# Attention scores and context of single tokens: from 128-wide block-diagonal products to 32 by 32 products in runs

## The reference, cut to what matters

```python
x = hidden                                     # (1, 2048, 1024)
n = layernorm(x)
q = (n @ wq.T + bq).reshape(B, S, 32, 32)      # k and v alike
scores = einsum('bshd,bstd->bsht', q, k) / sqrt(32)
context = einsum('bsht,bstd->bshd', softmax(scores), v).reshape(B, S, 1024)
x = x + context
x = x + ffn(layernorm(x))                      # w1, w2, w3 (2752 wide), each quantized
                                               # to 16 levels per block of 64 and back
```

## Time and profile before

| what | value |
|---|---|
| time, median of 3 runs | 1934.57 us (1934.41 to 1936.26) |
| the profiled execution's own time | 1933.85 us |
| its span | 1932.1 us |
| PE busy | 1883.0 us (97%) |
| DVE busy | 1730.8 us (90%) |
| ACT busy | 1542.4 us (80%) |
| POOL busy | 1256.0 us (65%) |
| one tile of the attention, in the loop | 30.6 to 30.7 us |

### The profile page before, as it was taken

One profiled execution on the slowest core, in us unless ns is written; L12 is line 12 of the kernel. 1 busy time (PEld: TensorE's weight loads), 2 busy tenths in 40 slices (PEclk: granted clock), 3 DMA queues, 4 the chain that ended last, 5 costly groups with the idle time before them and its releaser, 6 DMA issues.

```text
span 1932.1 us, 30875 instructions
## 1 busy us (share of the span) xinstructions
PE 1883.0 (97%) x10326; PEld 1053.0 (55%) x10326; DVE 1730.8 (90%) x1848; ACT 1542.4 (80%) x1779; POOL 1256.0 (65%) x707
## 2 busy tenths in 40 slices
PE   6899999999989999999999999999999999999998
PEld 5688888888764344444444444444444444444443
DVE  6789888888878999999999999999999999999995
ACT  7366757667568899898898998989989899898881
POOL 0134434343464797887877878778788797786971
PEclk9999999999989999999999999999999999999999
DMA  8435545455286422122122122122122122122114
GB/s 316 142 110 171 166 153 177 137 185 155 79 245 157 143 50 61 44 51 58 43 55 54 43 56 50 46 49 60 43 49 60 43 49 60 43 50 55 39 28 186
DMA packets 252861, 181.69 MB, mean 94 GB/s; under 512 B 177792, under 2 KB 220800, under 8 KB 252800
## 3 DMA queue, kind: packets, MB, share of 16 engines
q1 hardware_dynamic: 221600, 167.28, 30.9%
q10 hardware_dynamic: 31200, 13.64, 2.9%
HBM read 114.29 MB, written 24.12 MB: 72 GB/s over the span
## 4 chain that ended last, share of the span: by engine, by line
PE 64%; DVE 1%; issue 0%; DMA 0%; ACT 0%; SPq 0%; POOL 0%; DVEq 0%
PE bank L1907 42%; PE bank L1935 7%; PE bank L1936 7%; PE bank L1937 7%; PE bank L1933 0%; PE bank L1932 0%; DVE bank L1746 0%; DMA w3T_lo<-half 0%; DVE acc L1811 0%; DVE bank L1744 0%; SPq L1396 0%; DVE w_first L1746 0%; ACT half L1625 0%; ACT signs L1612 0%; DVE hidden L1754 0%
## 5 line engine op out<-in xcount | busy, mean ns | idle before, releaser
L1746 DVE SCALAR_TENSOR_TENSOR bank<-signs,bank 128x1024 f32<-128x1024 int8 (+2 forms) x756 | 920.3, 1217 | 54.6 <-ACT signs L1612 27.9
L1907 PE MATMUL bank<-x2T,w12T 128*128 128x512 f16 x4128 | 906.2, 380 | 11.9 <-DMA x2T<-x_lo_dram 9.0
L1907 PEld LDWEIGHTS bank<-x2T,w12T 128*128 128x128 f16 x4128 | 410.1, 99 | 493.3 <-DMA x2T<-x_lo_dram 9.2
L1612 ACT ACTIVATE signs<-w_first,compare_bias 128x1024 int8<-128x1024 f32 (+1 forms) x588 | 630.6, 1138 | 2.4 <-DVE bank L1746 1.9
L1612 ACT ACTIVATE signs<-w_last,compare_bias 128x1024 int8<-128x1024 f32 (+2 forms) x294 | 314.5, 1119 | 0.8 <-DVE w_first L1746 0.6
L1104 PE MATMUL bank<-wT,xT_hi 128*128 128x512 f16 x768 | 292.2, 381 | 2.4 <-PEq L321 2.4
L1104 PE MATMUL bank<-wT,xT_lo 128*128 128x512 f16 x768 | 292.0, 380 | 0.0
L1935 PE MATMUL bank<-w3T_hi,hT_hi 128*128 128x512 f16 x672 | 255.5, 380 | 7.3 <-DVE acc L1811 4.1
L1936 PE MATMUL bank<-w3T_lo,hT_hi 128*128 128x512 f16 x672 | 255.4, 380 | 0.0
L1937 PE MATMUL bank<-w3T_hi,hT_lo 128*128 128x512 f16 x672 | 255.3, 380 | 0.0
L1526 POOL TENSOR_TENSOR acc<-acc,hidden 128x512 f32<-128x512 f32 x160 | 200.8, 1271 | 28.0 <-ACT hidden L1653 27.2
(11 more groups left out here) (143 smaller groups left out, 2352.2 us busy)
## 6 DMA issues: line engine op xcount, KB each, us to landing
ff_raw<-in_L_ffn_w SPq DMA_DIRECT2D x63, 512.0 KB, 4.5
w_first<-in_L_ffn_w SPq DMA_DIRECT2D x41, 512.0 KB, 3.9
w_last<-in_L_ffn_w SPq DMA_DIRECT2D x19, 512.0 KB, 3.9
x_nat<-in_L_attn_hidden_states SPq DMA_DIRECT2D x16, 512.0 KB, 5.4
x_res<-in_L_attn_hidden_states SPq DMA_DIRECT2D x16, 512.0 KB, 4.6
x<-x_res SPq DMA_DIRECT2D x16, 512.0 KB, 3.0
acc<-x SPq DMA_DIRECT2D x4, 2048.0 KB, 9.1
out<-acc SPq DMA_DIRECT2D x15, 512.0 KB, 2.6
```

Source lines behind the costliest of these rows:

```text
L1612: nc.scalar.activation(signs[0:rows, ring(v, k), 0:cols], w_nat(v % SLOTS)[0:rows, 0:cols], ACT.Sign, scale=COMPARE[SUMMED[k]][0], bias=co ...
L1746: V.scalar_tensor_tensor(to, part, HALF_STEP[SUMMED[k]], total, ALU.mult, ALU.add).then_inc(sign_used, 1)
L1907: last = nc.tensor.matmul(dst, w, x[:, toks, c], start=c == 0 and i == 0, stop=c == C - 1 and i == 2)
```

## The change

Each product of 128x128 by 128x32 becomes four products of 32x32 by 32x32, one a quadrant, straight from `qT` and `flipped`. `diag`, its clearing, `place`, `place_q`, `place_probs` and their semaphores go; `flipped` and `qT` are read by TensorE itself. TensorE's waits change to `q_ready`, `p_ready` and `centered`; the wait of VectorE for `q_placed` goes. The products are not interleaved with the projections any more: all 128 score products of a tile stand in one run ahead of Q, 64 context products between K's halves, and 64 between K and V. In the opening 64 products follow each of slots 0, 8, 40 and 56. A semaphore increment on `held` stands ahead of each half.

```diff
-        diag = sb("diag", [P, QUAD, P])
-        MIX_FROM = 40
+        LAST_SCORES, LAST_MIXES = (0, C), (5 * C, 7 * C)
...
-            pool.memset(diag[:], 0.0).then_inc(diag_zero, 1)
...
-                    if not (it is None and n == 0):
-                        dve.wait_ge(q_placed, 2 * n)
...
-            def place(half, compact, done):
-
-                part = slice(half * HALF, (half + 1) * HALF)
-                for rows in quadrants:
-                    last = nc.scalar.activation(diag[rows, part, rows].rearrange("p (t u) h -> p t u h", u=2),
-                                                compact[rows, half * HALF // 2:(half + 1) * HALF // 2], ACT.Copy)
-                last.then_inc(done, 1)
...
                 if project:
                     pe.wait_ge(x_lo_done, 2 * n + 2)
-                    project_one(n, u, it, 0, with_lo, score if attend else None, (0, 2))
+                    if attend:
+                        score_part(n, end, 0, QUAD)
+                    project_one(n, u, it, 0, with_lo)
                 if normalize:
                     pe.wait_ge(normed, n + 2)
                     turn(x_nat[:, 1 - u], x_turned)
                 if project:
-                    project_one(n, u, it, 1, with_lo, mix if attend else None, (1, 2))
-                    project_one(n, u, it, 2, with_lo, mix_second if attend else None, (0, 1), ahead)
+                    project_one(n, u, it, 1, with_lo, mix_first if attend else None)
+                    if attend:
+                        mix_part(n, HALF, QUAD)
+                    project_one(n, u, it, 2, with_lo, ahead_half if ahead else None)
...
-                    if t % HALF == 0:
-                        pe.wait_ge(q_placed, 2 * n + half - 1)
+                    if t == 0:
+                        pe.wait_ge(q_ready, n)
                     if t % HALF == 0 and end and scores_of(n) is scores:
                         pe.wait_ge(ctx_read, 2 * n + half - 3)
-                    ins = nc.tensor.matmul(scores_of(n)[:, t], diag[:, t], kT[:, t // 2, :, t % 2], start=True, stop=True)
+                    if t % HALF == 0:
+                        pe.sem_inc(held, 1)
+                    for rows in quadrants:
+                        ins = nc.tensor.matmul(scores_of(n)[rows, t], qT[rows, t // 2, :, t % 2], kT[rows, t // 2, :, t % 2], start=True, stop=True)
...
-                        pe.wait_ge(p_placed, 2 * n + half - 1)
-                    ins = nc.tensor.matmul(context_of(n)[:, t], diag[:, t], vT[:, t // 2, :, t % 2], start=True, stop=True)
+                        pe.wait_ge(p_ready, 2 * n + half - 1)
+                        pe.wait_ge(centered, 2 * n + half - 1)
+                    if t % HALF == 0:
+                        pe.sem_inc(held, 1)
+                    for rows in quadrants:
+                        ins = nc.tensor.matmul(context_of(n)[rows, t], flipped[rows, t * HEADS:(t + 1) * HEADS], vT[rows, t // 2, :, t % 2],
+                                               start=True, stop=True)
```

More of the change, by code:

```diff
@@ L524, in attention @@
         mean_var2, var_eps2, rstd2 = norm2_row[:, 0:2], norm2_row[:, 2:3], norm2_row[:, 3:4]
-        diag_zero = sem("diag_zero")
         projected = sem("projected")
@@ L529, in attention @@
         q_ready = sem("q_ready")
-        q_placed = sem("q_placed")
         k_ready = sem("k_ready")
@@ L536, in attention @@
         p_ready = sem("p_ready")
-        p_placed = sem("p_placed")
         context_done = sem("context_done")
@@ L1007, in step @@
                     exponential(n, 0)
-                    place_probs(n, 0, end)
                 if feed:
@@ L1018, in step @@
                     turn_high2(act, n - 2)
-                if attend:
-                    place_probs(n, 1, end)
                 if end and not feed:
@@ L1024, in step @@
                     make_level(n, 1)
-                if project:
-                    place_q(n, 0, attend)
                 if end and not feed:
@@ L1030, in step @@
                     make_level(n, 2)
-                if project:
-                    place_q(n, 1, attend)
             def make_level(n, i):
@@ L1048, in exponential @@
                 nc.scalar.activation(flat, flat, ACT.Exp, scale=float(1 / np.sqrt(np.float32(HD)))).then_inc(exp_done, 1)
[L1050 to L1062, removed]
             def halve2(n):
@@ L1073, in tail @@
                 halve2(T - 2)
-                place_probs(T, 0, True)
                 next(feed)
@@ L1077, in tail @@
                 next(feed)
-                place_probs(T, 1, True)
                 next(feed)
@@ L1085, in tensor, with project_one @@
         def tensor(pe, feed_program):
-            def project_one(n, u, it, m, with_lo, between=None, share=(0, 2), halfway=None):
+            def project_one(n, u, it, m, with_lo, halfway=None):
                 for h in range(2):
@@ L1091, in project_one @@
                     if h == 1 and halfway:
-                        next(halfway)
+                        halfway()
                     to = bank[:, (6 * u + i) % PROJ_RING]
@@ L1106, in project_one, with mix_first, ahead_half @@
                             ins.then_inc(projected, 1)
-                        slot, slots = h * len(passes) + j, 2 * len(passes)
-                        if between and share[0] * slots <= 2 * slot < share[1] * slots:
-                            between((2 * slot - share[0] * slots) * HALF // slots, (2 * slot + 2 - share[0] * slots) * HALF // slots)
             def step(n, u, it, project=True, normalize=True, attend=True, end=True, feed=None, ahead=None,
                          with_lo=False):
[L1113 to L1120, removed]
+                def mix_first():
+                    mix_part(n, 0, HALF)
+                def ahead_half():
+                    next(ahead)
                 if project:
                     pe.wait_ge(x_lo_done, 2 * n + 2)
-                    project_one(n, u, it, 0, with_lo, score if attend else None, (0, 2))
+                    if attend:
+                        score_part(n, end, 0, QUAD)
+                    project_one(n, u, it, 0, with_lo)
                 if normalize:
@@ L1161, in attend_last @@
                 def attend_last(slot):
[L1164 to L1167, removed]
+                    if slot in LAST_SCORES:
+                        score_part(T, True, LAST_SCORES.index(slot) * HALF, (LAST_SCORES.index(slot) + 1) * HALF)
+                    elif slot in LAST_MIXES:
+                        mix_part(T, LAST_MIXES.index(slot) * HALF, (LAST_MIXES.index(slot) + 1) * HALF)
                 next(feed)
```

## The result

The changed kernel takes 1989.69 us (median of 4 runs, 1989.41 to 1990.67), the kernel before 1935.41 us beside it (1934.41 to 1936.59): a ratio of 1.0281, 95% interval 1.0263 to 1.0299. It is 54 us slower. The forecast was 2044 us, slower at 0.78, with 1905 to 2200 as its range. The direction held and the time lies inside the range, but the reason given was not the one found: that the time came out inside is luck.

What follows compares the result with a forecast made beforehand. The prediction took TensorE's own stream to bound each attention tile. 15 steps of +6.2 us for products and +1.0 for run edges, +108, plus 2 in the opening, gave +110 on 1933.85: 2044 us, range 1905 to 2200.

Steps and rivals of the forecast that it cites:

- What bounds the kernel now: Attention loop: a tile lasts as long as TensorE's stream, 30.6 to 30.7 us; VectorE next at 26.7, ScalarE's copies cost nothing.
- What a small product costs: Score and context products: 30 ns a step, 60 a product, 15.4 us in place of 9.2, +6.2 us a tile.
- the lower bound of 3.8: Products of a tile: four quadrants run beside each other, four products cost what one does; 3.8 us, -5.4 us a tile.
- signs of being wrong: Score run under 4.6 us or over 14, loop clock under 1.00, or PE waiting for q_ready, p_ready or ctx_read.
- rival 1: Score and context products: quadrants run side by side, VectorE's 26.7 us bound a tile, 1875 or about 1890 us; chance 0.11.
- the 34: Products in ns if different row groups start about 4 ns apart: 30 + 4, a tile's products 8.7 us, some 1941 us.
- The runs: Six changes a tile between small products and projections, each exposing 164 ns: +1.0 us a tile, bounds 0 and 2.
- Waits of the moved steps: Moved score and context runs: q_ready, p_ready and weigh come early enough, margins 2 to 3 us, so no wait added.
- The wait for x2T: Opening: PE's wait of 9.04 us would absorb +3.1 us of scores and shorten to about 6 us.
- The sum: Whole kernel: 15 steps of 6.2 + 1.0 give +108 us, the opening +2, in all +110 us, 2044 us.
- Rival 3: TensorE's sequencer: instructions limit at 28 ns each, a step 56 ns, a tile +19.5 + 1.0 us, about 2250 us; chance 0.12.
- Rival 4: Score runs of small products bring TensorE's clock down, 8 us a tile, +120, about 2165 us; chance 0.14.

Runs made afterwards that it cites:

- the order by quadrant: The change with, in each half, all 16 products of one quadrant before the next quadrant, instead of quadrants by turns: 2108.19 us, ratio 1.0894 to the kernel before.
- the kernel by quadrant with two runs: The change with products ordered by quadrant and a tile's scores in two runs of 64 products: 2080.02 us, ratio 1.0751 to the kernel before.
- two short runs written out: The change with scores in two runs of 64 products and TensorE's middle steps written out instead of looped: 1901.9 us, ratio 0.9838 to the kernel before.
- the body of 1440: The change with score and context operands cut to bf16, one load and one matmul a product: 1895.34 us, ratio 0.9783 to the kernel before.
- body of 1504: The change without the context's products but for one entry of 16, score run left as it was: 1901.63 us, ratio 0.9828 to the kernel before.
- the hybrid: Scores as in the change, context on the block diagonal as in the kernel before: 2024.32 us, ratio 1.0455 to the kernel before.

## Why the forecast was right in direction and wrong in its step

**What bounds the kernel now** held: TensorE's stream set the tile, ScalarE's 10 us a tile were worth nothing, and VectorE was next.

**What a small product costs** is the step that failed. The forecast took 30 ns a step and 256 x 0.060 = 15.4 us a tile; measured are 8.6 ns and 4.4 us, near the lower bound of 3.8. Of its own signs of being wrong, a score run under 4.6 us came true (2.52 us where it is not cut), and so did the lower clock; PE was not busy throughout. The 30 ns themselves were right, as the order by quadrant shows (29.5), and serial steps make a kernel of 2080 to 2108 us. Wrong was that consecutive steps are serial: the change visits the four quadrants by turns, and these overlap. The forecast had named this as rival 1 and gave it 0.11, on the ground that no matmuls of the trace share time; the trace of before had no two matmuls in different quadrants, so this was no evidence.

The Trainium skill ("TensorE: Matmul & The Clock Gate", Back-to-back issue gap) has a floor of about 25 ns from start to start; a run of 128 steps of 32x32 in 1.29 us stands against it, and the measurement decides; within one quadrant, at 29.5 ns, nothing here does. Its Part 3 on row groups was the right hint, and 8.6 ns a step, 17 a product, are below the 34 that the forecast worked out from it.

**The runs**: 1.0 us a tile was forecast for six edges; at 0.11 us (half of the 0.21 read in the kernel by quadrant with two runs) they cost 0.7.

**Waits of the moved steps** held: 0.7 us for flipped, none for q_ready, p_ready or ctx_read. The wait for x2T did not shrink to about 6 us, it stayed at 9.2.

**The sum** came nearer than its terms deserve, by luck: instead of +7.2 us a tile for products and edges there are -4.0 for these, +5.3 of idleness for instructions and +2 for the clock. **Rival 3** had instructions as the limit, but at the rate of the sequencer, and priced at 2250; the engine takes 5 ns each. The limit was the supply from memory, which no term of the forecast covered, though the instruction queue stood in the page. **Rival 4** had the clock fall through runs of small products: in the change it falls in the idle gaps (0.50 between 156 and 158 us), and with two short runs written out it stays at 1.00; by quadrant it falls within a busy run of 256 steps, 9.7 us long with the fall. So both causes exist, and the change met the first.

How it fits together: the loop's body was 928 loads and matmuls before and was brought in once; so were 1440 and 1504, while 1696 and 2464 are not kept. The records of the instruction queue's packets show it turn by turn. In the kernel before none begins between 164 and 485 us, with the body of 1440 none between 160 and 452. In the change 11 begin in each turn of the loop, in the hybrid with 1696 nine.

What is not kept comes in blocks of some 256 instructions. From gap to gap of one block in a score run pass 3.6 to 5.9 us (5.3 from 190.79 to 196.13), so 14 to 23 ns an instruction, of which the packet itself takes 0.9 to 1.9 us by its record. A tile's 1232 at that pace take 17 to 29 us, about as long as TensorE's 26.7 us tile if they are spread; but the 1120 between K's middle and the end of the next score run have only 15 us without gaps, and cannot be supplied in them. The pace alone is not the whole of it. In the hybrid the same stretch has 736 instructions in 17 us, which this pace would just bear, and its score runs stall for 76.8 us all the same. Blocks are not brought in far ahead: in the change the queue is idle between 143.9 and 151.3 us, and the score run at 151.14 then runs dry twice. So a dense run of 512 instructions, 2.5 us of work, outruns the few that are held. How many are held, and what a block's time is beside its packet, was not measured.

The Trainium skill ("Runtime: NRT & Kernel Launch", Instruction fetch mechanics) has blocks of 256 instructions, 16 KiB, fetched by the engine's own queue, and a loss at jumps out of the fetched window: 1.74 MB in 106 packets and 254 instructions between gaps agree, and so does the gap at the loop's jump. It gives TensorE room for 2048 instructions; if a whole body could stay in that room, the one of 1696 would have, and its nine packets a turn say that it did not. Where between 1504 and 1696 the limit lies, and whether other instructions than loads and matmuls make up the difference, was not tried, nor whether data transfers slow the fetch down.

## What to carry to other kernels

When an edit multiplies instructions, count those of the loop's body and those of the densest run, and look at the instruction queue of the page: a releaser "issue" in front of cheap work, at steps of a whole block, is the engine waiting for its own program. A body that is not kept can pay at each dense run; one that is kept pays only in the turn that brings it in. Small independent products should visit the quadrants by turns, in several short runs between large matmuls; here the same products cost 2108 us in one order, 1990 in another, and 1900 when spread and written out, 1.9% under the kernel before. A gap's price is not only its length: the clock behind it was worth, by the estimate above, another third.

## What was not expected of the hardware

- Steps of load and matmul, 32x32 f32, start 8.6 ns apart over four quadrants by turns, and 29.5 ns apart within one quadrant; in bf16, by turns, 7.5 to 9.4 ns.
- TensorE's clock fell from 2.4 to 1.2 GHz while it worked without a gap, in a run of 256 small steps taken by quadrant (0.50 from 178 us on, the run having begun at 173.6), and not in runs of 128 steps by turns of 1.29 us (1.00 from 202 to 231 us with two runs written out).
- A loop's body of 1504 loads and matmuls stays with the engine, with no instruction packet from 166.5 to 455.5 us; one of 1696 does not, with nine a turn.
- A block of 256 instructions reached TensorE 3.6 to 5.9 us after the one before it in dense runs, while its packet took 0.9 to 1.9 us.
